# Weighted values in an attention kernel: three products of 64 columns with one sum, in place of one of 128 and one of 64 with two sums

## The reference

```python
q = (x @ Wq).reshape(B, Nq, HEADS, DIM_HEAD)
k = (context @ Wk).reshape(B, context.shape[1], HEADS, DIM_HEAD)
v = (context @ Wv).reshape(B, context.shape[1], HEADS, DIM_HEAD)
sim = jnp.einsum('bihd,bjhd->bhij', q, k) * SCALE
attn = jax.nn.softmax(sim, axis=-1)
out = jnp.einsum('bhij,bjhd->bihd', attn, v)
out = out.reshape(B, Nq, HEADS * DIM_HEAD)
return out @ Wo + bo
```

## Time and profile before

| | |
|---|---|
| median of three runs | 919.01 us (918.77 to 920.0) |
| span of the profiled execution | 917.6 us |
| the profiled execution's own total | not given apart from its span; the median of the runs is 1.4 us above the span |
| instructions | 20100 |
| TensorE products | busy 98%, 7470 products |
| VectorE | busy 64% |
| ScalarE | busy 68% |
| POOL | busy 55% |

### The profile page before, as it was taken

The page is one execution under the profiler, slowest core; times in us unless marked ns, Lnnn a source line. Parts: engine busy times, 40 slices in busy tenths (PEclk is TensorE's granted clock), DMA queues, the critical chain, the costliest instruction groups (busy, mean ns, idle before and its releaser), DMA issues.

```text
span 917.6 us, 20100 instructions
## 1 busy us (share of the span) xinstructions
PE 903.4 (98%) x7470; PEld 564.5 (62%) x7470; DVE 590.5 (64%) x1069; ACT 628.3 (68%) x1398; POOL 504.8 (55%) x393
## 2 busy tenths in 40 slices
PE   6999999999999999999999999999999999999998
PEld 3556666666666666666666666666666455544444
DVE  6546666656666666666666666666667769886634
ACT  4857887777788788788878778877776523235540
POOL 4637656566556666666665655787777755310000
PEclk9999999999999999999999999999999999999999
DMA  9478677876767677677677868967999662333502
GB/s 333 98 142 167 135 129 141 163 145 139 136 142 131 135 146 138 132 137 141 134 143 152 157 130 140 194 133 146 186 190 165 105 133 64 72 86 74 183 13 80
DMA packets 340271, 126.38 MB, mean 138 GB/s; under 512 B 316113, under 2 KB 317905, under 8 KB 340177
## 3 DMA queue, kind: packets, MB, share of 16 engines
q1 hardware_dynamic: 325232, 96.66, 57.0%
q10 hardware_dynamic: 14944, 28.45, 9.6%
HBM read 45.36 MB, written 2.10 MB: 52 GB/s over the span
## 4 chain that ended last, share of the span: by engine, by line
PE 90%; DVE 3%; ACT 2%; SPq 2%; DMA 1%; issue 1%; ACTq 0%; DVEq 0%
PE v_ps L658 28%; PE k_ps L658 26%; PE e_ps L727 9%; PE e_ps L658 8%; PE o_ps L749 6%; PE o_ps L752 3%; PE e_ps L1014 3%; PE o_ps L1007 1%; PE e_ps L1007 1%; PE o_ps L768 1%; DMA raw<-in_ctx_t 1%; PE o_ps L947 1%; PE v_ps L1007 1%; DVE q_max L1531 1%; SPq L624 1%
## 5 line engine op out<-in xcount | busy, mean ns | idle before, releaser
L1984 POOL TENSOR_TENSOR p_l<-p_f,p_h 128x1024 f16<-128x1024 f32 x128 | 272.4, 2128 | 237.3 <-ACT p_f L1195 237.3
L1190 ACT ACTIVATE p_h<-e_ps,bias 128x512 f16<-128x512 f32 x256 | 175.7, 686 | 2.6 <-issue 0.5
L1195 ACT ACTIVATE p_f<-e_ps,bias 128x512 f32<-128x512 f32 x256 | 176.4, 689 | 0.0
L1526 DVE TENSOR_TENSOR k_l<-k_ps,k_h 128x512 f16<-128x512 f32 x128 | 88.5, 691 | 132.3 <-ACT k_h L1160 132.3
L1518 DVE TENSOR_TENSOR v<-v_ps,v 128x512 f16<-128x512 f32 x127 | 87.5, 689 | 107.0 <-ACT v L1152 107.0
L1531 DVE TENSOR_REDUCE q_max<-e_ps 128x2 f32<-128x1024 f32 x128 | 150.8, 1219 | 8.0 <-PE e_ps L727 0.9
L658 PE MATMUL v_ps<-wv_h,ctx_h 128*128 128x256 f16 x756 | 124.4, 273 | 1.2 <-DVE v L1518 1.1
L658 PE MATMUL v_ps<-wv_l,ctx_h 128*128 128x256 f16 x756 | 123.7, 273 | 0.0
L658 PE MATMUL v_ps<-wv_h,ctx_l 128*128 128x256 f16 x756 | 123.7, 273 | 0.0
L749 PE MATMUL o_ps<-v,pt_h 128*128 128x128 f16 x1024 | 104.2, 220 | 0.5 <-issue 0.5
L658 PE MATMUL k_ps<-ctx_h,wk_h 128*128 128x512 f16 x384 | 103.8, 379 | 0.0
(11 more groups left out here) (311 smaller groups left out, 1399.0 us busy)
## 6 DMA issues: line engine op xcount, KB each, us to landing
raw<-in_ctx_t ACTq DMA_DIRECT2D x26, 768.0 KB, 5.3
w_raw<-in_w_t SPq DMA_DIRECT2D x32, 256.0 KB, 3.8
raw<-in_ctx_t SPq DMA_DIRECT2D x5, 768.0 KB, 7.0
pt_h<-p_h SPq DMA_TRANSPOSE x128, 3.7
pt_l<-p_l SPq DMA_TRANSPOSE x128, 3.3
out<-xr SPq DMA_DIRECT2D x7, 256.0 KB, 2.0
x_in<-in_x SPq DMA_DIRECT2D x6, 256.0 KB, 11.0
o_all<-in_x ACTq DMA_DIRECT2D x6, 256.0 KB, 3.5
```

What stands on the lines that cost most here:

```text
L1190: act.activation(p_h[:, s % H_RING, h, :], e_ps[s % 2][:, h, :], ACT.Exp, scale=EXP_SCALE, bias=bias[:, n % 2, h, q:q + 1]).then_inc(p_hi, 1)
L1195: act.activation(p_f[:, s % F_RING, h, :], e_ps[s % 2][:, h, :], ACT.Exp, scale=EXP_SCALE, bias=bias[:, n % 2, h, q:q + 1], accum_out=p_su ...
L1526: dve.tensor_tensor(k_l[:, n % 2, cols], k_ps[:, :], k_h[:, n % 2, cols], ALU.subtract).then_inc(k_split, 1)
L1984: pool.tensor_tensor(p_l[:, s % L_RING, :, :], p_f[:, s % F_RING, :, :], p_h[:, s % H_RING, :, :], ALU.subtract).then_inc(p_split, 1)
```

## The change

The bank now holds one sum of 64 columns for each head. `pt_h` is multiplied by the 64 high columns and by the 64 low columns in two products, and `pt_l` by the 64 high columns in a third; all three add into the same 64 columns. Each of the three calls issues its own weight load. `accumulate` works on 64 columns in place of 128, `acc` is half as wide, `o_norm` has no first addition, and the counts on `o_step` go from three a stage to two. The buffer `o_sum` goes away. The buffers behind `acc` in memory move forward.

```diff
-        ("fade", [P, 2, 2, QUARTERS], F32), ("acc", [P, 2, 2, VW], F32), ("o_rec", [P, 2, 1], F32), ("o_sum", [P, 2, DH], F32),
+        ("fade", [P, 2, 2, QUARTERS], F32), ("acc", [P, 2, 2, DH], F32), ("o_rec", [P, 2, 1], F32),
...
-                        pe.matmul(acc_bank[:, h * VW:h * VW + VW], pt_h[:, s % T_RING, h * JT + j, :],
-                                  v[g][:, tile, 2 * (p % 2) + h, :],
+                        both, out_cols = v[g][:, tile, 2 * (p % 2) + h, :], slice(h * DH, h * DH + DH)
+                        pe.matmul(acc_bank[:, out_cols], pt_h[:, s % T_RING, h * JT + j, :], both[:, 0:DH],
                                   start=(j == 0 and h == 0), stop=False, skip_group_check=True)
-                        mm = pe.matmul(acc_bank[:, h * VW:h * VW + DH], pt_l[:, s % T_RING, h * JT + j, :],
-                                       v[g][:, tile, 2 * (p % 2) + h, 0:DH],
+                        pe.matmul(acc_bank[:, out_cols], pt_h[:, s % T_RING, h * JT + j, :], both[:, DH:VW],
+                                  start=False, stop=False, skip_group_check=True)
+                        mm = pe.matmul(acc_bank[:, out_cols], pt_l[:, s % T_RING, h * JT + j, :], both[:, 0:DH],
                                        start=False, stop=(j == JT - 1), skip_group_check=True)
                 mm.then_inc(pv_done, 1)
...
-                    new, total = o_ps[s % 2][:, h * VW:h * VW + VW], acc[:, n % 2, h, :]
+                    new, total = o_ps[s % 2][:, h * DH:h * DH + DH], acc[:, n % 2, h, :]
...
                 pool.wait_ge(o_rec_ready, 3 * n + 3)
-                pool.tensor_tensor(o_sum[:, :, :], acc[:, n % 2, :, 0:DH], acc[:, n % 2, :, DH:VW], ALU.add)\
+                pool.tensor_tensor(o_f[:, :, :], acc[:, n % 2, :, :], o_rec[:, :, :].broadcast_to([P, 2, DH]), ALU.mult)\
                     .then_inc(o_step, 1)
-                pool.wait_ge(o_step, 3 * n + 1)
-                pool.tensor_tensor(o_f[:, :, :], o_sum[:, :, :], o_rec[:, :, :].broadcast_to([P, 2, DH]), ALU.mult)\
-                    .then_inc(o_step, 1)
-                pool.wait_ge(o_step, 3 * n + 2)
+                pool.wait_ge(o_step, 2 * n + 1)
                 hi, lo = [o_half[:, b, i, p * P:p * P + P].rearrange("p (h d) -> p h d", h=2) for i in range(2)]
                 pool.tensor_copy(hi, o_f[:, :, :]).then_inc(o_step, 1)
-                pool.wait_ge(o_step, 3 * n + 3)
+                pool.wait_ge(o_step, 2 * n + 2)
                 pool.tensor_tensor(lo, o_f[:, :, :], hi, ALU.subtract).then_inc(o_ready, 1)
```

More of the change, by code:

```diff
@@ L160, in perceiver_kernel @@
     (o_all, ident, causal, bo_row, bv_row, b2_row, bq_col, bk_col, b1_col, b2_half, stats, mean_var, rstd, exponent,
-     q_max, bias, low, fade, acc, o_rec, o_sum, o_f,
+     q_max, bias, low, fade, acc, o_rec, o_f,
      ones, bq_half, bk_half, bias_prod, u_col, w_col, w_half, s_col, c_sum, c_col,
```

## The result

The changed kernel takes 921.50 us (median of eight runs, 920.72 to 923.6) against 919.24 us for the kernel before in the same measurement (eight runs, 918.12 to 920.45). The ratio is 1.003 with a 95% interval of 1.0021 to 1.0038: slower by 0.3% (by the two medians alone 2.26 us, 0.25%). The forecast was 921.4. One run of a later kernel, TensorE's part alone, took 946.65 us at a mean granted TensorE clock of 0.949 and is left out of the comparisons.

The account below looks back on a forecast made before the run. TensorE, almost never idle, was taken to bound the kernel: +2.56 us for third products less 0.2 us from shorter sums gave +2.4 on the 917.6 us span, 920.0, and with 1.4 us outside it 921.4; range 919.2 to 922.4.

Parts of the forecast that it names:

- The bound: Whole kernel: TensorE busy 903.4 of 917.6 us, and 675.3 of 677.0 us while all 128 slots run.
- The warning about busy time: Weighted-value products: the groups' 205 us counts overlaps for each group; the cost is the distance between starts.
- Part 1: Weighted values on TensorE: three products for two add 2.5 ns in each of 1024 tiles, 2.56 us.
- Part 2: Sums on VectorE and POOL: 58 ns less per VectorE sum, 14.5 us off POOL, hidden except 0.2 us.
- The credit of 0.2 us: TensorE's few waits for L1518: some hundredths saved in each, bounds 0 and 1.7 us.
- Part 3: ScalarE's fade, the queues' transposes and instruction fetch: no cost, since they wait for the same events as before.
- The sum: Whole kernel: +2.56 - 0.2 = +2.4 us on the 917.6 us span, plus 1.4 us outside it: 921.4.
- The weights rival: Weighted values: the fixed cost belongs to changing weights, so the tile stays at 85.0 ns; 918.8 us, chance 0.13.
- The relief on VectorE: TensorE's waits in the stretch vanish altogether: +2.56 - 1.7 = +0.9, 919.9 us, chance 0.07.
- The supply limit: Long blocks of weighted values: loads or instructions come no faster than 42.5 ns; 962.5 us, chance 0.03.
- The full overhead: Weighted values: each product needs 24.7 ns on top of its columns, 25.3 us in all; 944.3 us, chance 0.03.

Follow-up runs that it names:

- TensorE's part alone: The kernel before with only the 128-column product split into two of 64 into the two sums; VectorE still accumulates 128 columns, POOL still adds: 921.92 us, ratio 1.0031.
- the changed kernel again: The changed kernel, nothing altered, run once more for a second profile: 920.88 us, ratio 1.0027 to the kernel before.
- the other order: The changed kernel with its three products per tile ordered high by high, low by high, high by low: 922.14 us, ratio 1.0032 to the kernel before.
- the split values: The changed kernel with each 256-column product in value_tiles (first slot's excepted) as two of 128 with the same weights: 926.94 us, ratio 1.0084 to the kernel before.

## Why the prediction was right, step by step

- *The bound.* That TensorE sets the pace in the stretch of all slots was right. One product fewer or more moved the whole kernel by 27.0 and 28.4 us where its spacing alone gives 29.9.
- *The warning about busy time.* The groups give 103.0 to 103.1 us of busy time for each of the three lines now, 309 us by addition, where the blocks took 128 x 0.70 = 90 us. By the groups the change would have cost 104 us; it cost between 2 and 3.

```profile
L750 PE MATMUL o_ps<-v,pt_h 128*128 128x64 f16 x1024 | 103.0, 193 | 1.5 <-issue 1.5
...
L752 PE MATMUL o_ps<-v,pt_h 128*128 128x64 f16 x1024 | 103.1, 193 | 0.0
L754 PE MATMUL o_ps<-v,pt_l 128*128 128x64 f16 x1024 | 103.1, 193 | 0.0
```

- *Part 1.* 2.5 ns a tile and 2.56 us in all were forecast. The blocks of the trace grew by 2.5 ns a tile. The lowest runs differ by 2.60 us in the first measurement (920.72 and 918.12), and by 2.15, 2.14 and 2.14 us in the changed kernel again, TensorE's part alone and the other order. So even the lowest runs carry a few tenths of chance.
- *Part 2.* A saving of 58 ns on each of VectorE's sums was forecast; it is 67, as the row of L1555 shows, which answers to L1554 in the earlier trace rows. That it is hidden was right. The credit of 0.2 us was given to the wrong cause. Of the three waits of 1.1 us in all, one lies near 32 us, outside the stretch, and moves between 0.16 and 0.32 us from trace to trace. The two inside it were 0.42 and 0.43 us; they are 0.38 and 0.39 in the changed kernel, and the same with TensorE's part alone, where the sums are as wide as before. So the gain is about 0.1 us, and it comes from the longer blocks, which fill a little of each wait.

```profile
L1555 DVE SCALAR_TENSOR_TENSOR acc<-o_ps,fade,acc x192: 268/275/285, 70.1 to 741.2; 128x64 f32<-128x64 f32 x192
```

The first of the two waits, with TensorE's part alone:

```profile
609.67 0.49 PE L658 MATMUL v_ps<-wv_h,ctx_h 128*128 128x256 f16 x3 [0.38 <-DVE v L1521]
```

The reason given stands in the trace of after, in the timeline that answers to the earlier trace rows. VectorE's sums are done sooner, but the small product behind them (L1564) still ends when POOL's ctx_l ends, at 608.7, and L1519 starts only about then:

```profile
605.60 3.10 POOL L1975 TENSOR_TENSOR ctx_l<-raw,ctx_h 128x1536 f16<-128x1536 f32 x1
606.04 0.47 DVE L1555 SCALAR_TENSOR_TENSOR acc<-o_ps,fade,acc 128x64 f32<-128x64 f32 x2
606.43 2.29 DVE L1564 TENSOR_TENSOR p_faded<-p_sum,fade 128x8 f32<-128x8 f32 x1
608.64 0.68 DVE L1519 TENSOR_TENSOR v<-v_ps,v 128x512 f16<-128x512 f32 x1
...
609.47 0.49 PE L658 MATMUL v_ps<-wv_h,ctx_h 128*128 128x256 f16 x3 [0.38 <-DVE v L1519]
```

The sums, which read an accumulation bank, pass beside the same ctx_l at 0.47 us for two, and L1564, with two operands in SBUF, does not. The Trainium skill, SBUF — State Buffer, section "SBUF: two separate sides", states this as an exclusive lock between a POOL operation that reads SBUF and a VectorE operation with two SBUF inputs, held for the whole instruction; the trace agrees (L1564 takes 2.29 us, up to the end of ctx_l, where the shortest of its kind before took 156 ns).

- *Part 3.* The fetched instructions made no gaps in the blocks. But "at nothing" left something out. I looked for TensorE's waits at the end of the stretch in one trace and found 0.5 us, and did not see how full SP's queue is between 690 and 715 us. In that region the changed kernel waited 0, 1.0 or 2.5 us in the traces taken of it and of its reordered form, and its runs reach to 924.97 where those of the kernel before, beside them, end at 920.71. The half clock behind the longest wait adds to that in the traced execution; the other long runs were not traced. The medians of the changed kernel and of its two variants, 920.88 to 922.14, differ by up to 1.3 us, which these waits can account for. So the agreement of the total within 0.1 us is closer than the prediction's steps deserve: the medians themselves move by some tenths or more.
- *The sum.* The step from the span to the run's time was misread. In every execution for which both are on record the time lies 1.8 to 1.9 us above the span, not 1.4: the profiled execution of the kernel before had a span that belongs to about 919.4 us, above the median of 919.01. This does no harm, since adding 1.4 to its span is the same as adding the 2.4 us to the median.
- *The rivals.* The weights rival fell by the order of the products and by the split values. The relief on VectorE fell by the trace and by TensorE's part alone. The supply limit fell by blocks of 32 products at 29.2 ns. The full overhead fell by the blocks, 0.70 in place of 0.88 us, and by the total. The Trainium skill, TensorEngine Tiling (Array Packing), section Instruction Overhead, gives that rival when its 60 cycles are read as a cost on top of the columns; read as a floor, the page is borne out by the 25.3 ns of products of 32 columns.

What stays open: whether the changed kernel meets long waits near 700 us more often than the kernel before, and if so why, when each slot gives SP's queue 0.02 us more time. Two traces of each kernel are few; the runs are more: the changed kernel passed 922 us in five of 11 runs, the kernel before in none of the 21 beside them. The transposes of the weights take part in it, as moving them shows; slow landings take part too, as the table shows; what makes a landing slow was not tested. The 0.2 to 0.5 us by which the first block comes earlier in the traces of the changed kernel, its other order and TensorE's part alone (61.2 to 61.4 us in place of 61.5 to 61.7) have no reason on record either, since the programs do not differ on TensorE before that block. No kernel here beats the one before; the one with fewer products leaves out a term of the sum.

## What to carry to other kernels

Price a product on a TensorE that is never idle by the distance between starts: here 0.4167 ns a column plus 2.5 ns, with a floor near 25 ns. As an estimate from these two figures the floor binds under some 54 columns; the widths run here are 64 and more, which keep the law, and 32 and less, which lie on the floor. Splitting a wide product into halves of 64 or 128 columns was nearly free here, and still no gain while TensorE bounds: the work that it took from idle engines gave back nothing that could be measured. Before trusting a difference of 0.2%, look at the lowest runs and the spread as well as at the medians: waits on one tight queue moved medians here by half as much as the change. And when a wait near a block's start looks like one slow transfer, follow the block's own transfer from issue to landing: the slow one beside it may belong to the next block.

## What the runs showed of the hardware that was not expected

- Loading the same weights twice in a row costs the same as loading others: blocks of 699 to 700 ns with either order of products.
- Two products of 32 columns cost 50.5 ns where one of 64 costs 29.2.
- A DMA transpose can land late without holding its queue for long: the one issued at 694.98 us in the changed kernel run again held it for 1.34 us and landed 7.4 us after its issue, and TensorE lost 2.5 us by it. The median of such transposes lands after 3.1 us with no load on ScalarE's queue in flight, and after 4.6 us with one.
- A long wait of TensorE came with a slower stretch: the granted clock was 0.50 from 703.92 to 707.33 us, behind the wait of 2.53 us, and the stretch cost 1.6 us more. With one product fewer it was 0.50 from 691.5 to 694.9 us, around the end of a wait of 2.2 us. Behind waits of 1.0 and 1.8 us in other traces it stayed at 1.00.
